# Cross-attention keys turned by 16 VectorE block transposes a tile in place of four TensorE transposes

## What is computed

```python
qh = _layernorm((q @ Wq.T).reshape(B, Lq, H, D).transpose(0, 2, 1, 3), gq, bq) * scale
kh = _layernorm((k @ Wk.T).reshape(B, Lk, H, D).transpose(0, 2, 1, 3), gk, bk)
vh = (v @ Wv.T).reshape(B, Lk, H, D).transpose(0, 2, 1, 3)
attn = jax.nn.sigmoid(jnp.einsum('bhqd,bhkd->bhqk', qh, kh))
x = jnp.einsum('bhqk,bhkd->bhqd', attn, vh)
...
x = x.transpose(0, 2, 1, 3).reshape(B, Lq, C) @ Wp.T + bp     # q: normed x, k = v = context
```

## Time and profile before

| what | us |
|---|---|
| median of three runs | 2984.43 |
| lowest, highest | 2983.63, 2998.73 |
| the profiled execution, its own time | 2986.89 |
| its span | 2985.2 |
| cross-attention, start to the last copy of its sums | about 1988 |
| two tiles in steady state | 19.69 |
| VectorE / ScalarE / GpSimd busy in these 19.69 | 7.47 / 9.59 / 8.83 |

### The profile page before, as it was taken

How to read it: one execution, slowest core, us unless ns; L and a number is a source line. 1 busy time by engine, 2 the same in 40 slices (tenths; PEclk the granted TensorE clock), 3 DMA queues, 4 the chain that set the end, 5 groups by cost and what they waited for, 6 DMA issues and landing times.

```text
span 2985.2 us, 68957 instructions
## 1 busy us (share of the span) xinstructions
PE 2912.9 (98%) x28514; PEld 2357.5 (79%) x28514; DVE 1410.2 (47%) x1962; ACT 1463.9 (49%) x1450; POOL 883.8 (30%) x615
## 2 busy tenths in 40 slices
PE   5999999999999999999999999986999999999999
PEld 4777777777777777777777777754999998999998
DVE  5333333333333333333333333336558756657754
ACT  1445444444444444444444544431646555646554
POOL 3444444444444444444444444420000000000000
PEclk8999999999999999999999999997999999999999
DMA  5110000001001000000000000000545555555553
GB/s 205 29 28 25 27 25 28 28 25 28 25 28 28 25 28 25 28 28 25 25 27 28 28 25 25 21 29 29 184 171 191 183 193 194 195 186 184 184 184 134
DMA packets 53360, 231.64 MB, mean 78 GB/s; under 512 B 6056, under 2 KB 6312, under 8 KB 31920
## 3 DMA queue, kind: packets, MB, share of 16 engines
q1 hardware_dynamic: 53296, 230.74, 22.6%
HBM read 230.19 MB, written 0.52 MB: 77 GB/s over the span
## 4 chain that ended last, share of the span: by engine, by line
PE 93%; DVE 4%; issue 1%; ACT 1%; POOL 1%; DMA 0%; POOLq 0%; SPq 0%; DVEq 0%; ACTq 0%
PE kv_ps L1062 37%; PE f_ps L1321 22%; PE s_ps L1103 12%; PE o_ps L1115 12%; PE y_ps L1305 5%; PE kv_ps L1089 3%; PE pm L1188 1%; DVE w_lo L643 1%; DVE pre L930 0%; PE pm L1236 0%; ACT w_hi L533 0%; POOL k_var L437 0%; DMA wk_rows<-wk_dram 0%; PE kv_ps L1055 0%; PE pm L1177 0%
## 5 line engine op out<-in xcount | busy, mean ns | idle before, releaser
L493 ACT ACTIVATE even_probs<-s_ps 128x2048 f32<-128x2048 f32 x196 | 368.5, 1880 | 548.8 <-PE o_ps L1115 388.5
L437 POOL TENSOR_TENSOR k_var<-k_var,neg_half 128x16 f32<-128x16 f32 x196 | 571.1, 2914 | 15.5 <-POOL k_var L433 0.2
L427 POOL TENSOR_TENSOR ctx_lo<-ctx_raw,ctx_hi 128x512 fp32r<-128x512 f32 x196 | 253.5, 1293 | 769.1 <-DVE ctx_hi L686 769.1
L493 ACT ACTIVATE odd_probs<-s_ps 128x2048 f32<-128x2048 f32 x196 | 369.7, 1886 | 190.6 <-PE s_ps L1103 190.6
L643 DVE TENSOR_TENSOR w_lo<-w_raw,w_hi 128x2048 fp32r<-128x2048 f32 x160 | 366.4, 2291 | 175.1 <-ACT w_hi L533 174.9
L1321 PE MATMUL f_ps<-h_hi,w_hi 128*128 128x256 f32 x1536 | 428.8, 279 | 0.0
L1321 PE MATMUL f_ps<-h_lo,w_hi 128*128 128x256 f32 x1536 | 427.8, 279 | 0.0
L1321 PE MATMUL f_ps<-h_hi,w_lo 128*128 128x256 f32 x1536 | 427.8, 279 | 0.0
L533 ACT ACTIVATE w_hi<-w_raw 128x2048 fp32r<-128x2048 f32 x160 | 305.8, 1913 | 70.3 <-PE y_ps L1305 61.1
L694 DVE CAST kt_hi<-kv_ps 128x512 fp32r<-128x512 f32 x196 | 135.5, 692 | 428.4 <-PE kv_ps L1089 428.4
L705 DVE TENSOR_REDUCE k_var<-k_sq 128x16 f32<-128x512 f32 x196 | 134.4, 686 | 415.4 <-ACT k_sq L499 415.4
(11 more groups left out here) (197 smaller groups left out, 5130.2 us busy)
## 6 DMA issues: line engine op xcount, KB each, us to landing
w_raw<-w_dram SPq DMA_DIRECT2D x160, 1024.0 KB, 4.8
ctx_raw<-ctx_dram SPq DMA_DIRECT2D x196, 256.0 KB, 2.6
qkv_w<-qkv_w_dram SPq DMA_DIRECT2D x1, 3072.0 KB, 12.9
bias_rows<-bias_rows_dram SPq DMA_DIRECT2D x1, 1280.0 KB, 16.6
wq<-wq_dram SPq DMA_DIRECT2D x1, 1024.0 KB, 5.6
wk_rows<-wk_dram SPq DMA_DIRECT2D x1, 1024.0 KB, 7.6
wv<-wv_dram SPq DMA_DIRECT2D x1, 1024.0 KB, 9.7
out_w<-out_w_dram SPq DMA_DIRECT2D x1, 1024.0 KB, 17.7
```

The costliest lines, as they stand in the source:

```text
L427: g.tensor_tensor(ctx_lo[r % 2][:], raw[r % 4][:], ctx_hi[r % 2][:].bitcast(f32), ALU.subtract).then_inc(ctx_lo_made, 1)
L437: g.tensor_tensor(k_var[:, 2], k_var[:, 1], neg_half[:].to_broadcast([P, H]), ALU.pow)\
L493: s.activation(probs[r % 2][half][:], s_ps[:], ACT.Sigmoid).then_inc(probs_made, 1)
```

## The change

For each tile the four TensorE transposes and their waits go. VectorE does the turning with 16 transposes, each of a block of 32 context rows by 4 groups by 32 components: block (b, q) reads partitions 32b to 32b+31 of `k_n`, and writes the 32 partitions of quarter q of a new SBUF tile `k_rows`. The split into `kt_hi` and `kt_lo` then reads `k_rows` in SBUF where it read `kv_ps` in PSUM, and the projections no longer wait for `kt_lo_made`.

`k_rows` has one buffer. The first transpose of a tile waits for the split of the tile before (`kt_lo_made`, on the same engine). VectorE's list is written in a new order: everything of one tile (sum, norm, values, cast of tile t+2, 16 transposes, split) before anything of the next. So the norm [709 in the new numbering] now stands right behind the sum [702] whose deviations it needs from GpSimd. GpSimd's and ScalarE's lists are the same as before.

```diff
-            def split_turned(it, r):
-                dve.wait_ge(t_made, n_of(it, r, 1, 1))
+            def split_keys(it, r):
+                dve.wait_ge(k_blocked, n_of(it, r, HG * HG, HG * HG))
                 wait(dve, s_made, n_of(it, r, 2, -2))
-                turned = turned_in(r).rearrange("p (g k) -> p g k", g=NG)
                 hi, lo = kt_hi[r % 2][:], kt_lo[r % 2][:]
-                v.tensor_copy(hi, turned).then_inc(kt_hi_made, 1)
+                v.tensor_copy(hi, k_rows[:]).then_inc(kt_hi_made, 1)
                 dve.wait_ge(kt_hi_made, n_of(it, r, 1, 1))
-                v.tensor_tensor(lo, turned, hi.bitcast(f32), ALU.subtract).then_inc(kt_lo_made, 1)
+                v.tensor_tensor(lo, k_rows[:], hi.bitcast(f32), ALU.subtract).then_inc(kt_lo_made, 1)
...
+            def turn_keys(it, r):
+                dve.wait_ge(k_normed, n_of(it, r, 1, 1))
+                wait(dve, kt_lo_made, n_of(it, r))
+                for b in range(HG):
+                    keys = slice(D * b, D * (b + 1))
+                    for q in range(HG):
+                        v.transpose(k_rows[D * q:D * (q + 1), :, keys],
+                                    k_n[keys].rearrange("p (g q) d -> p q g d", g=NG)[:, q]).then_inc(k_blocked, 1)
+
             def two_tiles(it, r):
-                normalise(it, r - 1)
-                high_part(it, r + 1)
-                sum_squares(it, r)
-                split_turned(it, r - 1)
-                normalise(it, r)
-                copy_values(it, r)
-                split_turned(it, r)
-                high_part(it, r + 2)
-                sum_squares(it, r + 1)
-                copy_values(it, r + 1)
+                for t in (r, r + 1):
+                    sum_squares(it, t)
+                    normalise(it, t)
+                    copy_values(it, t)
+                    high_part(it, t + 2)
+                    turn_keys(it, t)
+                    split_keys(it, t)
...
@@ (TensorE)
-            def turn_keys(it, r, last=False):
-                pe.wait_ge(k_normed, n_of(it, r, 1, 1))
-                if r % 2:
-                    pe.wait_ge(k_kept, n_of(it, r, 1, 1 if last else 2))
-                else:
-                    pe.wait_ge(v_copied, n_of(it, r, 1, 1))
-                for grp in range(NG):
-                    ins = t.transpose(turned_in(r)[:, grp * P:(grp + 1) * P],
-                                      k_n[:, HG * grp:HG * grp + HG].rearrange("p h d -> p (h d)"), ident[:])
-                ins.then_inc(t_made, 1)
```

More of the change, by code:

```diff
@@ L137, in perceiver_block @@
         early_probs = [sb(f"even_probs{i}", [P, HG, 2, TOK], f32, first_slots) for i in range(2)]
+        k_rows = sb("k_rows", [P, NG, P], f32, first_slots)
         first_slots.close()
@@ L256, in perceiver_block @@
         k_normed = sem("k_normed")
-        t_made = sem("t_made")
+        k_blocked = sem("k_blocked")
         kt_hi_made, kt_lo_made = sem("kt_hi_made"), sem("kt_lo_made")
@@ L286, in n_of @@
             return it * (4 * per) + (per * r + more)
-        def turned_in(r):
-            return kv_ps[:, 1 - r % 2]
         def is_first(it, r, t):
@@ L710, in normalise @@
                 dve.wait_ge(k_dev_made, n_of(it, r, 1, 1))
-                wait(dve, t_made, n_of(it, r))
+                wait(dve, k_blocked, n_of(it, r, HG * HG))
                 v.tensor_tensor(k_n[:, :, 0:D - 1], k_c[:, :, 0:D - 1], per_row(k_var[:, 2], D - 1), ALU.mult)\
                     .then_inc(k_normed, 1)
-            def two_tiles(it, r):
-                normalise(it, r - 1)
-                high_part(it, r + 1)
-                sum_squares(it, r)
-                split_turned(it, r - 1)
-                normalise(it, r)
-                copy_values(it, r)
-                split_turned(it, r)
-                high_part(it, r + 2)
-                sum_squares(it, r + 1)
-                copy_values(it, r + 1)
+            def turn_keys(it, r):
[6 more added lines that the diff above has]
+                                    k_n[keys].rearrange("p (g q) d -> p q g d", g=NG)[:, q]).then_inc(k_blocked, 1)
+            def two_tiles(it, r):
+                for t in (r, r + 1):
[5 more added lines that the diff above has]
+                    split_keys(it, t)
             dve.wait_ge(once("consts"), 1)
@@ L771, in _ @@
             copy_values(0, 0)
-            split_turned(0, 0)
             high_part(0, 2)
+            turn_keys(0, 0)
+            split_keys(0, 0)
             sum_squares(0, 1)
+            normalise(0, 1)
             copy_values(0, 1)
+            high_part(0, 3)
+            turn_keys(0, 1)
+            split_keys(0, 1)
             two_tiles(0, 2)
@@ L781, in _ @@
             two_tiles(nq - 1, 6)
-            normalise(nq, 3)
-            split_turned(nq, 3)
             dve.wait_ge(av_made, 2 * (NKT + 1))
@@ L1072, in projection @@
                         wait(pe, k_kept, n_of(it, r))
-                        if r % 2:
-                            wait(pe, kt_lo_made, n_of(it, r, 1, -1))
                     if m == 12:
                         wait(pe, v_copied, n_of(it, r))
-                        if r % 2:
-                            wait(pe, kt_lo_made, n_of(it, r))
                     project(it, r, m // 12, m % 12 // 3, m % 3)
-            def turn_keys(it, r, last=False):
-                pe.wait_ge(k_normed, n_of(it, r, 1, 1))
-                if r % 2:
-                    pe.wait_ge(k_kept, n_of(it, r, 1, 1 if last else 2))
-                else:
-                    pe.wait_ge(v_copied, n_of(it, r, 1, 1))
-                for grp in range(NG):
-                    ins = t.transpose(turned_in(r)[:, grp * P:(grp + 1) * P],
-                                      k_n[:, HG * grp:HG * grp + HG].rearrange("p h d -> p (h d)"), ident[:])
-                ins.then_inc(t_made, 1)
             def scores(it, r, half):
@@ L1121, in two_tiles @@
                 projection(it, r, 0, 24)
-                turn_keys(it, r - 1)
                 scores(it, r - 2, 0)
@@ L1127, in two_tiles @@
                 scores(it, r - 2, 1)
-                turn_keys(it, r)
                 projection(it, r + 1, 0, 12)
@@ L1152, in _ @@
             pe.sem_inc(w_used, 2)
-            turn_keys(0, 0)
             projection(0, 1, 0, 24)
@@ L1158, in _ @@
                 two_tiles(it, 6)
-            turn_keys(nq, 3, last=True)
             scores(nq, 2, 0)
```

## The result

The changed kernel takes 3425.07 us (median; 3424.27 to 3428.66) against 2984.88 us before. It is slower by a factor of 1.1465 (95% interval 1.143 to 1.150), that is by 440 us. Its profiled execution has a span of 3426.9 us. The copy of the attention's sums starts at 2426.5 us, where it started at 1987.6, so 439 us of the loss lie in the attention.

The account below looks back on a forecast made before the run. VectorE's list was taken to become the bound in place of TensorE: 6.62 + 16 x 0.33 = 11.90 us a tile over 195 tiles, 398 us more than 2986.9, so 3385 us, range 3100 to 3560.

Parts of the forecast that it names:

- VectorE's list becomes the path: In the attention loop, VectorE's operations for one tile need 11.90 us against 9.33 on TensorE and so set the pace.
- P = 6.62 + 16x: VectorE's time per tile: 6.62 us of other steps plus 16 transposes, x from one start to the next; 11.90 at 0.33.
- Sum to norm, 4.05: VectorE, start of the sum to start of the norm: it waits out GpSimd's whole part, 4.05 us a tile.
- Norm, values, cast, 0.59 + 0.60 + 0.33: VectorE's start-to-start times per tile in us: norm 0.59, copy of the values 0.60, cast of tile t+2 0.33.
- `kt_hi` from SBUF, 0.45, and `kt_lo`, 0.60: VectorE's split: `kt_hi` reading SBUF takes 0.45 us with its dependent follower, `kt_lo` 0.60 with an independent one.
- The transposes, 16 x 0.33 = 5.28: VectorE's 16 transposes per tile start 0.33 us apart, as 128-element router operations with dependent followers do; 5.28 us together.
- The total: From tile 1's sum at 58.0, 195 tiles of 11.90 us; copy of the sums at 2385.7, 398 us later; 3385 us.
- Held or overlapping: Transposes changing quarter: held, 0.33 us apart (3260 to 3555, chance 0.64), or fully overlapping, 0.205 (near 2995, 0.05).
- TensorE's floor: TensorE's own need without its transposes: 19.69 - 1.03 = 18.66 us per two tiles, 9.33 a tile.
- The rival of 2886: TensorE stays the bound and the removed transposes' 101 us are gained: 2886 us, needing x below 0.169; chance 0.05.
- The stop once per body and its clock: TensorE stands still about 5.2 us per two tiles, waiting for the values' copy; cold stretches after each gap cost nothing.
- the rival on the clock: TensorE's clock stays at half for whole bodies, 37.3 us per two tiles, 4713 us in all; chance 0.04.

Follow-up runs that it names:

- the extra matmuls: The changed kernel with the 12 key matmuls of each even tile, from tile 4 on, done twice: 3424.34 us.
- GpSimd's 2.7 us: The changed kernel with GpSimd's power replaced by an addition of the same shape (0.21 us in place of 2.91): 2896.22 us.
- the cheaper transposes: The changed kernel with each block kept within its own quarter: 16 transposes, 3094.32 us; four transposes of all 128 partitions, 2897.36 us.
- the values' 0.60 us: The changed kernel with the copy of the values alone moved between the sum and the norm: 3311.03 us.
- the two runs that reached the floor: The changed kernel with four transposes of 128 partitions a tile, 2897.36 us, and with GpSimd's power replaced by an addition, 2896.22 us.

## Why the prediction was right

I forecast 3385 us in a range of 3100 to 3560, and 3425 was measured. Step by step:

- **VectorE's list becomes the path.** Right. The waits changed sides as described, and the extra matmuls cost nothing.
- **P = 6.62 + 16x.** Right in form. Taken off one at a time, GpSimd's 2.7 us, the cheaper transposes and the values' 0.60 us each came out as the sum says, within some hundredths of a us a tile, until TensorE's floor was reached.
- **Sum to norm, 4.05.** Measured 4.05 in three tiles of four and 4.15 in the fourth, 0.025 more on average.
- **Norm, values, cast, 0.59 + 0.60 + 0.33.** Measured the same to 0.01.
- **`kt_hi` from SBUF, 0.45, and `kt_lo`, 0.60.** Measured 0.46 and 0.61.
- **The transposes, 16 x 0.33 = 5.28.** The start-to-start time is 0.333, as taken. That it came so close is in part luck. I took the 0.33 of a follower that needs the result, a record of 0.29 and a gap of 0.04; here it is a record of 0.302 and a gap of 0.031, of which 0.017 go with the semaphore that each transpose raises. With the pause before the cast the block is 5.43, 0.15 more.
- **The total.** These differences make 0.195 us a tile, 12.095 in place of 11.90. The copy of the sums was forecast for 2385.7 and starts at 2426.5, 40.8 us later. Of these 195 x 0.195 = 38 us are the tiles, 2.4 the tail at the lower clock, and 2.1 the last tile's norm of 2.78 us. About 1.3 go off for the two casts and the seven pauses that the tiles outside the loop lack, and 0.2 since tile 1's sum starts at 57.77 and not at 58.0.
- **Held or overlapping.** I took the held value, for which the trace of before had no row. That choice carried the forecast: within one quarter the transposes do overlap, at 0.20, and 16 x 0.20 would have put the time near 2995, no change. The rule of the Trainium skill, page "VectorE: DVE Perf Modes", section "Two Vector instructions with no wait between them", says that an instruction is held when its input or its output starts in another quarter than the last one's. The trace agrees for both: 0.333 apart with either change, 0.20 with neither. The reason I gave beside it, that a transpose must fill a block first, was wrong as a cost: nothing of the 0.03 us shows.
- **TensorE's floor.** A mis-sized term without effect on the result: 9.33 us a tile by my sum, 9.42 measured, since the key projection that stood behind the removed transposes takes 2.95 us in place of 2.77. The rival of 2886 would have been about 2897, as the two runs that reached the floor show.
- **The stop once per body and its clock.** The spare time was right, 5.35 us against 5.2. The stop itself is shorter, 3.5 us on average, since the clock falls to 0.56 behind it and the slower matmuls use up the rest, as the rival on the clock had it. In the loop this costs nothing. In the tail, which I left at 7.1 us, it costs 2.4.

## What to carry to other kernels

Before work is moved to an engine that looks half idle, add up its list for one round from start to start, with the waits for other engines' answers that its order exposes. VectorE was busy for 7.47 of 19.69 us, yet the new list needed 12.1 us a tile where 9.8 were to be had. The same operations need 8.7 in an order that puts the transposes where GpSimd is being waited for. When an operation is moved earlier, ask also what it releases on another engine, and beside which operation that will then run.

## What was not expected of the hardware

- The norm of two SBUF inputs took 1.69 us when it started 0.13 us after GpSimd's subtraction of 1.28 us. In the kernel before, the last tile's norm took 2.75 us from 1967.89, beside an addition of GpSimd from 1967.77 that lasted 2.34. Transposes beside the same subtraction, from 1006.72 to 1007.99 in the changed kernel, were not slowed: the 16 took 5.30 us, as with no operation of GpSimd beside them (from 2410.46).
- A semaphore raised by a short VectorE instruction cost 0.017 us each, where the instructions were held one behind the other.
- A VectorE transpose of 128 four-byte elements per partition has a start-to-start time of 0.20 us within one quarter or over all 128 partitions, and 0.333 when either the input's or the output's quarter changes. Each of these raised a semaphore.
